# Part x by channels from the DRAM input instead of by transposes, with the norm's mean in the weights, and a reordered opening and last slot

## The reference

```python
x = x + attn(_layernorm(x))      # q, k, v = n @ W.T ; decay ; y ; group norm ; @ W_o.T
x = x + ffn(_layernorm(x))       # (silu(n@sw1+sb1) * (n@sw3+sb3)) @ sw2 + two experts with gelu
def _layernorm(x): m = mean(x); v = var(x); return (x - m) / sqrt(v + 1e-5)
```

## Time and profile before

| | us |
|---|---|
| median of three runs | 437.23 |
| the profiled execution | 437.39 |
| its span | 435.6 |
| TensorE busy | 427.2 (98%) |
| VectorE busy | 328.6 (75%) |
| ScalarE busy | 216.6 (50%) |
| GpSimd busy | 74.5 (17%) |

### The profile page before, as it was taken

How to read it: one execution, slowest core, us unless ns; L and a number is a source line. 1 busy time by engine, 2 the same in 40 slices (tenths; PEclk the granted TensorE clock), 3 DMA queues, 4 the chain that set the end, 5 groups by cost and what they waited for, 6 DMA issues and landing times.

```text
span 435.6 us, 14430 instructions
## 1 busy us (share of the span) xinstructions
PE 427.2 (98%) x6270; PEld 385.4 (88%) x6270; DVE 328.6 (75%) x789; ACT 216.6 (50%) x416; POOL 74.5 (17%) x69
## 2 busy tenths in 40 slices
PE   6999999999999999999999999999999999999996
PEld 5899999999999999998989988899888999888995
DVE  6887778766878768976798887978879878746423
ACT  3466656546763567535337335473344734346430
POOL 1103223522145013550520000100001000000000
PEclk9999999999999999999999999999999999999999
DMA  7443332232331121325520015100142001120011
GB/s 268 146 147 100 101 102 75 76 84 78 122 116 52 52 99 53 99 100 164 176 96 2 1 50 198 43 0 1 48 155 86 0 0 49 48 96 2 0 50 48
DMA packets 15384, 34.66 MB, mean 80 GB/s; under 512 B 2368, under 2 KB 2656, under 8 KB 14816
## 3 DMA queue, kind: packets, MB, share of 16 engines
q1 hardware_dynamic: 14896, 33.05, 22.8%
q10 hardware_dynamic: 432, 0.79, 0.6%
HBM read 25.44 MB, written 8.40 MB: 78 GB/s over the span
## 4 chain that ended last, share of the span: by engine, by line
PE 90%; DVE 3%; ACT 3%; DMA 2%; issue 1%; ACTq 0%; POOL 0%; DVEq 0%
PE bank L371 50%; PE bank L380 14%; PE bank L381 7%; PE bank L450 6%; PE bank L493 4%; PE bank L480 3%; PE bank L464 3%; DMA wqkv_raw<-wattn 2%; PE bank L429 1%; PE bank L390 1%; ACT vexp L688 1%; ACT kexp L688 1%; PE bank L511 1%; DVE pm L885 1%; PE bank L574 0%
## 5 line engine op out<-in xcount | busy, mean ns | idle before, releaser
L371 PE MATMUL bank<-x2hi,sw_hi 128*128 128x512 f32 x128 | 51.3, 400 | 0.0
L371 PE MATMUL bank<-x2lo,sw_hi 128*128 128x512 f32 x128 | 50.4, 394 | 0.0
L371 PE MATMUL bank<-x2hi,sw_lo 128*128 128x512 f32 x128 | 50.3, 393 | 0.0
L703 ACT ACTIVATE keo<-kT,msk 128x512 f32<-128x512 f32 x32 | 21.4, 715 | 51.8 <-DVE kT L874 51.8
L380 PE MATMUL bank<-w_both,ehi 128*128 128x512 f32 x128 | 46.4, 397 | 0.0
L380 PE MATMUL bank<-sw_both,ghi 128*128 128x512 f32 x128 | 46.3, 394 | 0.0
L775 ACT ACTIVATE sil<-bank,s1b 128x512 f32<-128x512 f32 x32 | 22.0, 688 | 46.6 <-PE bank L371 46.6
L1049 DVE STREAM_TRANSPOSE x2t<-xl 32x256 f32<-32x256 f32 x96 | 41.8, 436 | 1.8
L885 DVE TENSOR_TENSOR pm<-bank,msk 128x512 f32<-128x512 f32 x64 | 39.5, 678 | 2.5 <-PE bank L450 2.5
L371 PE MATMUL bank<-xhi,wqkv_hi 128*128 128x256 f32 x128 | 38.2, 298 | 1.3 <-DVE xlo L869 1.2
L794 ACT ACTIVATE ehi<-xres 128x512 fp32r<-128x512 f32 x32 | 20.2, 633 | 32.9 <-PE bank L381 32.4
(11 more groups left out here) (124 smaller groups left out, 1103.9 us busy)
## 6 DMA issues: line engine op xcount, KB each, us to landing
xin<-xa SPq DMA_DIRECT2D x16, 256.0 KB, 2.9
w_raw<-w SPq DMA_DIRECT2D x16, 256.0 KB, 3.3
xres<-xs SPq DMA_DIRECT2D x16, 256.0 KB, 3.3
x_scratch<-xres SPq DMA_DIRECT2D x16, 256.0 KB, 3.0
xl<-x_scratch SPq DMA_DIRECT2D x8, 512.0 KB, 4.3
xr<-x_scratch SPq DMA_DIRECT2D x4, 1024.0 KB, 4.8
out<-xr SPq DMA_DIRECT2D x7, 512.0 KB, 2.6
sw_raw<-sw SPq DMA_DIRECT2D x6, 256.0 KB, 3.8
```

What stands on the lines that cost most here:

```text
L371: mm = nc.tensor.matmul(o, w[c][l], x[c][r], start=first and c == 0 and j == 0, stop=last and c == n - 1 and j == 2)
L703: cp = nc.scalar.activation(keo[:, :, :, odd, :], kT[:].rearrange("p g (c j) -> p c g j", c=CPS), ACT.Copy, scale=parity[:, odd:odd + 1])
```

## The change

- For parts 2 to 15, x is loaded a second time, by channels (`xt`, 256 KB a part, into `xin_t`). The transposes on TensorE and the rounding on ScalarE of those parts are gone. `ln_apply` of those parts is gone too.
- The norm's mean is put into the weights once: matmuls with a matrix of -1/256 give the negative column means in PSUM (`weight_means`), VectorE adds them to the raw weights (`centre_w`), before the split into halves.
- The norm's factor of a part goes out from `ln_r` to DRAM (128 partitions, 8 bytes each) and comes back as a row on all partitions (128 x 1 KB). VectorE multiplies `xin_t` by it (`scale_x`), copies to `xhi` and subtracts to `xlo` (`split_x`, after the last product that reads the old `xhi`).
- ScalarE in s = 1 does `high_y` before the output bias; VectorE does the residuals before `ln2_apply`.
- SyncE waits for other points of TensorE's program (k_done, q_done, v_done) and issues the new transfers there. GpSimd waits for `xlo_ready` before its weight work.
- The opening: part 0 is loaded in two halves by the two queues, the identity comes ahead of the other masks, the k weight goes to SyncE's queue, decays are loaded in two halves; part 0 is transposed, rounded and split in halves, after the k weight's means; `decay_k(0)` goes ahead of `ln_apply(1)`.
- `slot_bias` has another place in SBUF, so it is loaded after phase one, ahead of the store of the last quarter of x1, and added beside gates 6 and 7 of batch 0.
- The last slot of the last batch is a `split_product` into 256 columns, with one addition behind it.

```diff
-WARM_UP = (5, 2)
+WARM_UP = 4
 # SyncE, step(h)
                 sp.wait_ge(sc_done, h + 1)
+                if h and h + 2 < PARTS:
+                    load_rstd(h + 2)
...
-                sp.wait_ge(s_done, h + 1)
+                if h + 1 < PARTS:
+                    sp.wait_ge(k_done, h + 2)
...
+                if h + 1 < PARTS:
+                    sp.wait_ge(q_done, h + 2)
+                if h + 3 < PARTS:
+                    load_xt(h + 3)
                 sp.wait_ge(y_done, h + 1)
...
+                if h + 3 < PARTS:
+                    store_rstd(h + 3)
 # SyncE, new
+            def store_rstd(h):
+                sp.wait_ge(ln_rstd, h + 1)
+                sp.dma_start(rstd_dram[h].rearrange("(p t) -> p t", t=TILES), ln_r[:]).then_inc(rstd_stored, 16)
+            def load_rstd(h):
+                sp.wait_ge(rstd_stored, (h - 1) * 16)
+                if h >= 4:
+                    sp.wait_ge(x_scaled, h - 3)
+                sp.dma_start(rstd_row[h % 2][:], rstd_dram[h].partition_broadcast(P)).then_inc(rstd_landed, 16)
 # TensorE
+            def weight_means(i):
+                pe.wait_ge(w_landed[(1, 0, 2)[i]], 16)
+                for c in range(CB):
+                    mm = nc.tensor.matmul(p_bank[i][:, 0:D], minus_mean, wqkv_split.raw[:, (1, 0, 2)[i], c, :], start=(c == 0), stop=(c == CB - 1))
+                mm.then_inc(wmean_done, 1)
...
                     k_by_tokens(h + 1)
                     project_v(h + 1)
-                    if h + 2 < PARTS:
-                        transpose_x(h + 2)
                     scores(h + 1)
...
+                if isinstance(b, int) and s == NE - 1:
+                    split_product(o_bank[s % 2][:, 0:D], g, [(x[:, 0, :], x[:, 1, :]) for x in w]).then_inc(slot_done, 1)
+                else:
+                    wide_product(o_bank[s % 2][:], g, w).then_inc(slot_done, 1)
...
-            warm_up(WARM_UP[0])
-            pe.wait_ge(msk_landed, 16)
-            transpose_x(0)
-            warm_up(WARM_UP[1])
+            warm_up(WARM_UP)
+            pe.wait_ge(mean_set, 1)
+            weight_means(0)
+            pe.wait_ge(ident_landed, 16)
+            for t in range(TILES):
+                pe.wait_ge(xn_ready, t + 1)
+                for c in range(CB):
+                    mm = nc.tensor.transpose(x0_bank[t][:, c * P:(c + 1) * P], xin[0][:, t, c * P:(c + 1) * P], ident)
+                mm.then_inc(t_done, 1)
+            weight_means(1)
+            weight_means(2)
             project_k(0)
 # ScalarE, step(h)
+                high_y(h)
                 if b and s == 1:
                     copy_bias(b - 1, p_bank[1])
-                high_y(h)
...
-                if h + 2 < PARTS:
-                    high_x(h + 2)
 # VectorE, step(h) and new
+                if h + 2 < PARTS:
+                    scale_x(h + 2)
                 low_y(h)
                 y_sums(h)
-                if h + 3 < PARTS:
-                    ln_apply(h + 3)
-                else:
-                    ln2_apply(0, h + 3 - PARTS)
...
+                if h + 3 >= PARTS:
+                    ln2_apply(0, h + 3 - PARTS)
                 if h + 2 < PARTS:
-                    low_x(h + 2)
+                    split_x(h + 2)
...
+            def scale_x(h):
+                x = xin_t[h % 2]
+                dve.wait_ge(xt_landed[h % 2], h // 2 * 16)
+                dve.wait_ge(rstd_landed, (h - 1) * 16)
+                x = x[:].rearrange("p c (t n) -> p c t n", t=TILES)
+                row = rstd_row[h % 2][:].rearrange("p (n t) -> p t n", t=TILES)
+                nc.vector.tensor_tensor(x, x, row.unsqueeze(1).broadcast_to([P, CB, TILES, P]), ALU.mult).then_inc(x_scaled, 1)
+            def split_x(h):
+                dve.wait_ge(x_scaled, h - 1)
+                dve.wait_ge(v_done, h)
+                nc.vector.tensor_copy(xhi[:], xin_t[h % 2][:]).then_inc(xhi_ready, 1)
+                dve.wait_ge(xhi_ready, h + 2)
+                nc.vector.tensor_tensor(xlo[:], xin_t[h % 2][:], xhi[:].bitcast(F32), ALU.subtract).then_inc(xlo_ready, 1)
+            def centre_w(i):
+                dve.wait_ge(wmean_done, i + 1)
+                raw = wqkv_split.raw[:, (1, 0, 2)[i]]
+                nc.vector.tensor_tensor(raw, p_bank[i][:, 0:D].unsqueeze(1).broadcast_to([P, CB, D]), raw, ALU.add).then_inc(w_centred, 1)
 # VectorE, opening
-            low_w(0)
+            centre_w(0)
+            for t in range(TILES):
+                dve.wait_ge(xhi_ready, t + 1)
+                at = slice(t * P, (t + 1) * P)
+                nc.vector.tensor_tensor(xlo[:, :, at], x0_bank[t][:, 0:CB * P].rearrange("p (c t) -> p c t", c=CB),
+                                        xhi[:, :, at].bitcast(F32), ALU.subtract).then_inc(xlo_ready, 1)
+            low_w(0)
+            centre_w(1)
+            centre_w(2)
             low_w(1)
-            low_x(0)
+            ln_sums(1)
             low_w(2)
-            ln_sums(1)
+            dve.wait_ge(deck_landed, 16)
+            decay_k(0)
             ln_apply(1)
```

More of the change, by code:

```diff
@@ L129, in moe_retention @@
             xin = [sb_1(f"xin{i}", [P, TILES, D]) for i in range(NSUP)]
+            xin_t = [sb_1(f"xin_t{i}", [P, CB, SUPER]) for i in range(2)]
+            rstd_row = [sb_1(f"rstd_row{i}", [P, SUPER]) for i in range(2)]
             dec = sb_1("dec", [P, 2, GROUPS, SUPER])
@@ L170, in moe_retention @@
         x2t = sb("x2t", [P, CB, T])
+        slot_bias = sb("slot_bias", [P, NE, D])
         def const(name):
@@ L344, in _ @@
                 load_xl(1, half)
+            for j in range(3):
+                store_x1(last, j)
+            sp.wait_ge(bias_stored, 16)
+            sp.wait_ge(o_done, NBATCH * 4)
+            sp.wait_ge(xres_biased, NBATCH * 4)
             for j in range(4):
-                store_x1(last, j)
+                load_slot_bias(j)
+            store_x1(last, 3)
             for j in range(4):
@@ L677, in _, with high_x1 @@
         def _(act):
-            def high_x(h):
-                act.wait_ge(t_done, h + 1)
+            def high_x1():
+                act.wait_ge(t_done, 3)
+                act.wait_ge(v_done, 1)
                 nc.scalar.activation(xhi[:].rearrange("p c t -> p (c t)"), b_bank[:], ACT.Copy).then_inc(xhi_ready, 1)
@@ L799, in experts @@
                         high_x2(b + 1, j)
-            for i in (1, 0, 2):
+            act.dma_start(xin[0][:, 1, :], xa[0, :, 1, :]).then_inc(x0_landed, 16)
+            for i in (1, 2):
                 act.dma_start(wqkv_split.raw[:, i], wattn[:, i]).then_inc(w_landed[i], 16)
             for i in (1, 0, 2):
-                act.wait_ge(w_landed[i], 16)
+                act.wait_ge(w_centred, (1, 0, 2).index(i) + 1)
                 nc.scalar.activation(wqkv_split.hi[:, i], wqkv_split.raw[:, i], ACT.Copy).then_inc(whi_ready, 1)
-                if i == 0:
-                    high_x(0)
+                if i == 1:
+                    for t in range(TILES):
+                        act.wait_ge(t_done, t + 1)
+                        nc.scalar.activation(xhi[:, :, t * P:(t + 1) * P], x0_bank[t][:, 0:CB * P].rearrange("p (c t) -> p c t", c=CB),
+                                             ACT.Copy).then_inc(xhi_ready, 1)
             act.wait_ge(msk_landed, 16)
             spread_k(0)
-            high_x(1)
             act.wait_ge(kexp_cleared, 1)
             copy_k(0)
+            high_x1()
             act.wait_ge(v_cleared, 2)
@@ L851, in ln_sums, with ln_rest @@
                     st = nc.vector.bn_stats(ln_st[:, t, :], x[:, t, :])
+                ln_rest(h, st)
+            def ln_rest(h, st):
                 st.then_inc(ln_stats, 1)
@@ L1086, in add_slot @@
                 dve.wait_ge(slot_done, b * NE + (s + 1))
+                if isinstance(b, int) and b == last and s == NE - 1:
+                    nc.vector.tensor_tensor(xr[:, s, :], o_bank[s % 2][:, 0:D], xr[:, s, :], ALU.add).then_inc(o_ready, 1)
+                    return
                 nc.vector.tensor_tensor(xr[:, s, :], o_bank[s % 2][:, 0:D], xr[:, s, :], ALU.add).then_inc(o_half, 1)
@@ L1141, in _ @@
                 nc.vector.memset(vexp[i][:], 0.0).then_inc(v_cleared, 1)
-            ln_sums(0)
+            for t in range(TILES):
+                dve.wait_ge((x_landed[0], x0_landed)[t], 16)
+                st = nc.vector.bn_stats(ln_st[:, t, :], xin[0][:, t, :])
+            ln_rest(0, st)
             ln_apply(0)
+            def centre_w(i):
+                dve.wait_ge(wmean_done, i + 1)
+                raw = wqkv_split.raw[:, (1, 0, 2)[i]]
+                nc.vector.tensor_tensor(raw, p_bank[i][:, 0:D].unsqueeze(1).broadcast_to([P, CB, D]), raw, ALU.add).then_inc(w_centred, 1)
             def low_w(i):
@@ L1324 @@
         "xa": x_chunks,
+        "xt": x.reshape(PARTS, SUPER, CB, P).transpose(0, 3, 2, 1),
         "xs": x_slots,
```

92 lines of the change are left out of this document (56 added, 36 removed).

## The result

The changed kernel takes 448.46 us (median of six runs, 445.41 to 450.88), the kernel before beside it 437.14 (436.67 to 437.95). The ratio is 1.0256, interval 1.0217 to 1.0295. The forecast was 432.4, with 435.2 as the upper end of its range. The profiled execution took 445.41, the quickest of the six; its span is 443.6, against 435.6 before.

What follows compares the result with a forecast made beforehand. TensorE was taken to bound the kernel, busy 427.2 of 435.6 us. Terms 5.7 + 0.6 - 0.5 + 0.2 - 1.5 + 0.4 = 4.9 off the profiled 437.39 gave 432.5, 432.4 as median; range 430.9 to 435.2.

Steps and rivals of the forecast that it cites:

- waits for nothing new: Plain steps of phase one: VectorE's copy and subtraction fit beside the scores (1.94 us), so no new wait.
- rival C: Factor's row comes back late in each step; at 11.0 us for the trip, thirteen steps lose 9.1, time 441.6; chance 0.05.
- waits in steps 5 and 9: project_k's waits for `xlo` in s = 1, 0.29 us each, go with `high_y` ahead of the output bias: 0.6 gained.
- Steps 0 to 12: Phase one: transposes between v and the scores go, 0.44 us a step, 13 x 0.44 = 5.7 gained.
- A: Phase one: ScalarE's copies become the limit, 0.10 us of slack; 2.6 less gain, 435.0; chance 0.22 together with B.
- B: Ahead of the scores: transposes covered a tile-shape gap, saving 0.3 a step; 1.8 less gain, 434.2; chance 0.22 together with A.
- The copy of 512 elements: VectorE's copy to `xhi`: taken as 0.6 us; an estimated 0.35 by the skill's rule.
- Step 13: Phase one, beside the second norm: project_k waits about 1.2 us for `xlo`; 0.5 lost, bounds 0.2 to 0.6.
- The opening: Start of kernel: project_k(0) at 10.2, q and v wait 0.5 each; 1.5 us lost, bounds +0.3 and -2.3.
- Step 14: Scores of part 15 no longer wait for the residual, now ahead of `ln2_apply`: 0.2 us gained.
- the last slot: End of kernel: one addition fewer (0.46 us), TensorE 0.08 more; 0.4 gained.
- the later load of `slot_bias`: After phase one: there by 225, first use about 228, so 0; if its four transfers run serially, 4 us uncovered.

Runs made afterwards that it cites:

- e1: The changed kernel without the 14 stores of the factor, its rows loaded from `sb2` instead: 435.22 us, ratio 0.9949.
- e6: The kernel before plus 13 transfers of `ln_r` in 8-byte pieces into two partitions of SBUF, read by nobody: 437.40 us, ratio 1.0002.
- e10: The changed kernel with neither the stores of the factor nor the loads of its row (rows are ones): 433.88 us, ratio 0.9912.
- e2: The changed kernel with the stores kept but no row loaded (rows are ones): 450.57 us, ratio 1.0324.
- 4: The kernel before plus 13 stores of `ln_r` to DRAM as in the change, read by nobody: 445.24 us, ratio 1.0153.
- e3: The changed kernel with `xt` loaded for parts 2 and 3 alone, later parts reading old data: 448.14 us, ratio 1.0223.
- e5: The changed kernel with `ln_r` transposed on VectorE, so the factor leaves as 8 pieces of 128 bytes a part: 434.97 us, ratio 0.9944.
- 9: The kernel of e5 with `split_x` ahead of `ln2_apply` in step 13: 439.09 us, ratio 1.0020.
- 12: The kernel of run 9 with GpSimd's additions of step 13 placed behind `ln2_apply`: 434.79 us, ratio 0.9917.

## Why the prediction was wrong, and where it was right

**The step that failed is the cost of the stores.** The prediction asked of them only whether the row is back in time (a plain step "waits for nothing new", and rival C). C priced the trip, and there it came out: the store took about 5 us, not 7.1, the row 3.7, and `scale_x` waited once, 1.84 us at 27.80, without effect on TensorE. What the prediction put at nothing, without a reason, is what a store does to everything else: 13 us (448.46 against 435.22 in e1), where the whole gain was to be 4.9. The row that C took its price from, `gn_w` with 7.1 for 1 KB, could not have told: it is a load into SBUF, and in e6 the 8-byte pieces that went into SBUF cost nothing.

The sum of the failure, from the starts of the state sums and the spans of three profiled runs:

| | before | e10 | after |
|---|---|---|---|
| state sums of step 1 | 27.88 | 29.56 | 29.86 |
| from there to step 15's | 163.86 | 157.82 | 169.85 |
| from there to the end | 243.86 | 243.42 | 243.89 |
| span | 435.6 | 430.8 | 443.6 |

After against e10 is the price of stores and rows: 12.8 us, of which 12.0 lie in phase one. The gaps in that stretch sum to 9.0, the slow clock behind the longest is 1.5, and 0.7 goes off, since project_k(15) does not wait there. About 2.2 remain. Compared start by start, e10's matmuls and these say where: five of the gaps delay TensorE by 0.20 to 0.28 more than their idle time shows, 1.2 together, and at three more places it loses 0.27, 0.38 and 0.40 with hardly any idle time. Elsewhere the two keep the same pace. The profiled execution is the quickest of six, so the medians give a higher price: 448.46 - 433.88 = 14.6. Runs 1 and 10 split it by ratios: 0.9949 - 0.9912 = 0.37%, 1.6 us, for the rows; 1.0256 - 0.9949 = 3.1% for the stores.

The Trainium skill, "DMA: Bandwidth & Descriptors", section "Specifications", which the prediction weighed, says that pieces under 512 bytes are done as read-modify-write. The runs agree for 8 bytes against 512 into DRAM (445.24 and 437.72); that it is a read-modify-write, no run shows. They add that 8-byte pieces into SBUF cost nothing (437.40), and that 8 pieces of 128 bytes a part, also under 512, cost little (434.97). The section has nothing on what such writes do to others.

Before against e10 is the rest of the change, term by term. Steps are counted here by TensorE's program, from the state sums of one part to those of the next; the prediction's waits in steps 5 and 9 fall at the start of TensorE's steps 6 and 10.

**Steps 0 to 12, 0.44 each: right.** The scores follow v at once. The chain after, part 7's neighbourhood:

```profile
100.49 0.44 PE bank L486 x4
100.92 1.43 PE bank L423 x12
102.35 1.94 PE bank L507 x64
```

In the earlier trace rows the 0.44 of L390 stood between. The intervals of state sums in e10 are 9.91 to 9.92 in steps 2 and 3, where they were 10.34 and 10.35; 12.83 where 13.27. The thirteen steps gave 5.73 together, forecast 5.7. Some luck is in it: step 1 gave 0.23 alone, and step 9 0.73, since e10 has a small stall in the one and the kernel before has one in the other (118.94, in the middle of its state sums). Rivals A and B fall: no wait for `vexp`, no longer gap ahead of the scores. (A's price did not follow from its slack either: 0.2 us more against 0.10 of slack is 0.1 a step, 1.3 and not 2.6.) The copy of 512 elements takes less than the 0.6 that I took:

```profile
173.58 0.43 DVE L959 CAST xhi<-xin_t 128x512 fp32r<-128x512 f32 x1
```

The Trainium skill, "VectorE: DVE Perf Modes", section "Mode 2×_2P — use both read ports for one tensor", has the rule for one source from which the prediction estimated 0.35. The row is nearer to that than to my 0.6, and the subtraction of the same size with two sources takes 0.69. I had discarded the rule because a one-source operation on 256 elements takes 0.40, but a fixed part in each instruction would leave room for both; no run separates it.

**Waits in steps 5 and 9, 0.29 each: right.** Intervals 13.55 and 13.56 became 12.82 and 12.83, 0.73 = 0.44 + 0.29.

**Step 13, -0.5: too dear by 0.4.** From the state sums of part 13 to those of part 15 it was 24.61 before and is 24.44 in e10, 0.17 less. Step 14's gain of 0.24 is in it, so step 13 itself lost 0.07. In e10 the timelines of VectorE and TensorE show:

```profile
172.91 1.37 DVE L1123 TENSOR_SCALAR xl<-xl,ln_mv,ln_r 128x256 f32<-128x256 f32 x4
174.19 0.42 DVE L954 CAST xhi<-xin_t 128x512 fp32r<-128x512 f32 x1
174.65 0.69 DVE L956 TENSOR_TENSOR xlo<-xin_t,xhi 128x512 fp32r<-128x512 f32 x1
...
175.39 0.38 PE L418 MATMUL bank<-xhi,wqkv_hi 128*128 128x256 f32 x1 [0.71 <-DVE xlo L956]
```

A wait of 0.71, not 1.2: `ln2_apply` starts 0.34 later after the state sums of part 13 than before (9.97 against 9.63), not 0.6, the copy is 0.2 shorter, and between copy and subtraction 0.04 pass, not 0.1.

**The opening, -1.5: too small by 0.5.** TensorE's timeline after, to be laid beside the earlier trace rows:

```profile
10.60 0.36 PE L423 MATMUL bank<-xhi,wqkv_hi 128*128 128x256 f32 x1 [1.03 <-DVE wqkv_lo L1251]
...
19.54 0.39 PE L423 MATMUL bank<-xhi,wqkv_hi 128*128 128x256 f32 x1 [0.59 <-DVE xlo L943]
```

The chain of the k weight rules, as said, but project_k(0) starts at 10.60, not 10.2 (9.8 to 11.0 in the other runs with centred weights). The waits for q and v are 0.23 and 0.15 (at 12.50 and 14.35), not 0.5 each; part 1's `xlo` costs 0.59, not 0.4. from_scores(0) starts at 23.61, 2.0 later than before, not 1.5; in e10 it is 2.1. That it comes 13.0 after project_k(0), as forecast (12.95), is luck, with the two waits 0.6 cheaper. Over the runs with centred weights it lies 1.2 to 2.4 behind.

**Step 14, 0.2, and the last slot, 0.4: right.** The scores of part 15 no longer wait for the residual (0.24). From the state sums of part 15 to the end it is 0.44 less, the last slot's; the later load of `slot_bias` cost nothing, as forecast. The last addition stands alone at the end, where the earlier trace rows had two:

```profile
440.90 0.42 DVE L1179 TENSOR_TENSOR xr<-bank,xr 128x256 f32<-128x256 f32 x1 [1.96 <-PE bank L423]
```

The sum of the terms came out by luck: step 13 was 0.4 better than forecast and the opening 0.6 worse, so that e10's span is 430.8 against 430.7. By its median (0.9912 x 437.23 = 433.4) e10 gains 1 us less than forecast, 3.8 and not 4.9. The kernel that needs the row for real pays the row's 1.6 on top.

## What to carry to other kernels

Before a result makes a detour through DRAM, count the bytes of a piece that one partition writes. Two floats a partition, 8 bytes, cost 13 us here; turned on an engine first, they leave as a few longer pieces. And a transfer on a queue has two prices: when it lands, and what it does to other traffic, that of the instructions included; where TensorE is 98% busy, the second can be the larger, and no semaphore shows it, only idle time put down to issue in the middle of a group. To tell such gaps from others, count the matmuls between them, and look in the DMA view for slices in which nothing starts.

When an instruction of VectorE is moved, look at what GpSimd does in its new place.

## What the runs showed of the hardware

- A store of 128 pieces of 8 bytes into DRAM takes about 5 us (issued at 26.75, the load behind it at 31.27). Thirteen of them cost 6.7 us (by the ratio) in a kernel that never stops for them, fourteen cost the changed kernel 13 us. The 256 KB loads of x in these kernels land in 5.0 to 5.4 us in the median, not 2.9. In the four kernels with such stores 69 to 80 DMA packets take over 1.5 us, in the others 1 to 3. The same pieces into SBUF, or pieces of 512 bytes into DRAM: no time that the comparison can tell.
- In the changed kernel TensorE stands still for 0.2 to 2.4 us at a time (4.13 at most in e2), mostly in the middle of a group and often several us after the last store. That the stores cause most of it is shown by runs 1 and 4. That it is instructions that come late is shown by the places: in the changed kernel the gaps lie 127 matmuls or a multiple of it apart, within one; e1, e2, e3 and e5 have all or most of theirs at the same matmuls; and each gap of the changed kernel ends 1.1 to 1.7 us after a packet of instructions landed. No run takes the fetching away. How a store leads to a gap that begins up to 10 us later is open.
- After the gap of 2.37 us the granted clock went from 1.00 to 0.50, the level of 1.2 GHz, for 3.4 us; TensorE had been idle from 65.95 to 68.32. After the other gaps of that trace, 1.63 us and less, it stayed at 1.00.
- A one-source operation of VectorE on float32 in SBUF took 1.37 instead of 0.40 us beside GpSimd's additions, and 1.38 for all four when GpSimd waited (runs 9 and 12). The Trainium skill, "SBUF — State Buffer", section "SBUF: two separate sides", says that the two engines share a pair of ports, held by one of them for a whole instruction. Both runs agree: each held instruction lasts as long as one of GpSimd's.
